# The query and key projection of a channel attention as two row tiles without zero blocks, in a two-bank PSUM area

## The reference

```python
def _L0_conv_ref(x, wq, bq, wk, bk, wv, bv):
    xf = x.reshape(b, c_in, h * w)
    q = jnp.einsum('oc,bcn->bon', wq, xf) + bq[None, :, None]
    k = jnp.einsum('oc,bcn->bon', wk, xf) + bk[None, :, None]
    v = jnp.einsum('oc,bcn->bon', wv, xf) + bv[None, :, None]
    attn = jnp.einsum('bcn,bdn->bcd', q, k) / jnp.sqrt(c)
    attn = jax.nn.softmax(attn, axis=-1)
    attended = jnp.einsum('bcd,bdn->bcn', attn, v)
    return x + attended.reshape(b, c, h, w)
```

## Time and profile before

| | |
|---|---|
| median of 3 runs | 303.3 us (303.17 to 304.55) |
| span of the profiled execution | 301.8 us, 7399 instructions |
| PE | 287.8 us busy (95%) |
| PEld | 183.7 us (61%) |
| DVE | 213.0 us (71%) |
| ACT | 190.4 us (63%) |
| POOL | 53.0 us (18%) |
| DMA | 4.98 MB, mean 16 GB/s |

### The profile page before, as it was taken

How to read it: one execution, slowest core, us unless ns; L and a number is a source line. 1 busy time by engine, 2 the same in 40 slices (tenths; PEclk the granted TensorE clock), 3 DMA queues, 4 the chain that set the end, 5 groups by cost and what they waited for, 6 DMA issues and landing times.

```text
span 301.8 us, 7399 instructions
## 1 busy us (share of the span) xinstructions
PE 287.8 (95%) x2870; PEld 183.7 (61%) x2870; DVE 213.0 (71%) x424; ACT 190.4 (63%) x399; POOL 53.0 (18%) x139
## 2 busy tenths in 40 slices
PE   7798999999999999999999999999999999989995
PEld 3555567567555765575767566675565656657742
DVE  3173984779799788858877827687998996655342
ACT  1268757867886569837685654866975755564332
POOL 0332040400140215010222100301421011011110
PEclk9999999999999999999999999999999999999999
DMA  7300000000000000100010001000000000000001
GB/s 235 140 0 20 0 22 2 2 0 2 0 2 3 3 1 2 35 2 0 3 35 2 3 0 31 8 2 1 2 2 0 21 0 3 17 2 0 2 17 35
DMA packets 3057, 4.98 MB, mean 16 GB/s; under 512 B 336, under 2 KB 2768, under 8 KB 2896
## 3 DMA queue, kind: packets, MB, share of 16 engines
q1 hardware_dynamic: 3024, 4.52, 4.7%
HBM read 3.47 MB, written 1.05 MB: 15 GB/s over the span
## 4 chain that ended last, share of the span: by engine, by line
PE 85%; DVE 5%; ACT 5%; issue 3%; POOL 1%; ACTq 0%; POOLq 0%; DVEq 0%
PE ps_cv L534 22%; PE ps_pair L615 11%; PE ps_yb L494 8%; PE ps_pair L480 7%; PE ps_ma L437 6%; PE ps_ma L464 4%; PE ps_mb L580 3%; PE ps_pair L602 3%; PE ps_pair L570 3%; PE ps_mb L591 3%; PE ps_mb L547 3%; PE ps_mb L388 2%; PE ps_pair L635 2%; PE ps_mb L624 2%; PE ps_yb L374 1%
## 5 line engine op out<-in xcount | busy, mean ns | idle before, releaser
L901 DVE TENSOR_TENSOR sb_wt<-ps_yb,sb_xe 128x512 f32<-128x512 f32 x144 | 94.0, 684 | 26.4 <-PE ps_xb L489 24.9
L534 PE MATMUL ps_cv<-sb_wt,sb_w_x 128*64 128x256 f32 x576 | 77.3, 385 | 0.0
L740 ACT ACTIVATE sb_xe<-ps_xb 128x512 f32<-128x512 f32 x72 | 43.0, 597 | 19.3 <-PE ps_xb L489 19.2
L534 PEld LDWEIGHTS ps_cv<-sb_wt,sb_w_x 128*64 128x64 f32 x576 | 38.2, 136 | 20.2 <-issue 7.5
L615 PE MATMUL ps_pair<-sb_y_pad,sb_par 64*128 64x256 f32 x320 | 37.4, 383 | 0.3 <-ACT sb_gates L799 0.3
L615 PEld LDWEIGHTS ps_pair<-sb_y_pad,sb_par 64*128 64x128 f32 x320 | 30.9, 184 | 5.8 <-issue 2.5
L942 DVE SCALAR_TENSOR_TENSOR sb_dw_acc<-sb_z_pad,sb_par,sb_dw_acc 128x256 f32<-128x256 f32 x56 | 25.2, 480 | 9.4 <-ACT sb_dw_acc L792 5.3
L494 PE MATMUL ps_yb<-sb_hats,sb_sel 32*128 32x512 f16 x144 | 29.8, 383 | 0.7
L1039 POOL TENSOR_TENSOR sb_parts<-sb_hat,sb_parts 128x256 f16<-128x256 f32 (+2 forms) x40 | 23.3, 615 | 38.7 <-ACT sb_parts L710 38.6
L1046 POOL TENSOR_SCALAR sb_sc<-sb_mv 128x1 f32<-128x1 f32 x16 | 3.0, 190 | 142.1 <-DVE sb_mv L936 74.7
L489 PE MATMUL ps_xb<-sb_hats,sb_sel 32*128 32x512 f16 x72 | 27.7, 385 | 0.2 <-ACT sb_hats L719 0.2
(11 more groups left out here) (117 smaller groups left out, 438.4 us busy)
## 6 DMA issues: line engine op xcount, KB each, us to landing
sb_par<-in_par SPq DMA_DIRECT2D x1, 1519.5 KB, 7.7
sb_x_in<-in_x SPq DMA_DIRECT2D x8, 128.0 KB, 2.1
out_y<-sb_y_out SPq DMA_DIRECT2D x8, 128.0 KB, 1.7
sb_par<-in_par SPq DMA_DIRECT2D x1, 397.0 KB, 4.0
sb_par<-in_par SPq DMA_DIRECT2D x1, 192.0 KB, 3.4
sb_par<-in_par SPq DMA_DIRECT2D x1, 128.0 KB, 2.2
sb_sel<-in_sel SPq DMA_DIRECT2D x1, 128.0 KB, 3.9
```

The costliest lines, as they stand in the source:

```text
L534: mm = nc.tensor.matmul(cv[C * b:C * (b + 1), 0:PIX], w_x[n % 2][:, b, h, k, :], wt_of(n, k, h)[:, PIX * b:PIX * (b + 1)], start=(k == 0 a ...
L740: nc.scalar.activation(xe[t % XE][:, :], xb[:, :], ACT.Copy).then_inc(ev("xe_ok"), 1)
L901: nc.vector.tensor_tensor(wt_of(n, k, h)[:, :], yb[h][:, :], xe[t % XE][:, :], ALU.mult)\
```

## The change

`qk` leaves the steps of `mb` and joins those of `pair`. Its matmuls become row tiles: for each half of 128 pixels and each image of the pair, the 64 rows of that image are the stationary operand with all 128 pixels as columns, and the 64 x 128 block of `qk_w` that is not zero is the moving one. The two images write different banks. The count of matmuls stays four, with 128 moving columns each in place of 256. DVE's addition reads both banks, four runs of 128 columns, and writes the same `qk_sb`. The lists of steps are not changed.

```diff
--- before.py
+++ after.py
@@ -123,9 +123,9 @@
 }
 
 
-BANK = {"mb": ("prep", "qk", "attn", "at", "mix", "x1", "qk2", "v2", "et0", "et1", "av", "fuse",
+BANK = {"mb": ("prep", "attn", "at", "mix", "x1", "qk2", "v2", "et0", "et1", "av", "fuse",
                "ff2"),
-        "pair": ("wx0", "wx1", "wx2", "logit", "gate", "scan", "ff")}
+        "pair": ("qk", "wx0", "wx1", "wx2", "logit", "gate", "scan", "ff")}
 DONE = {"prep": "prep_ok", "qk": "qk_ok", "attn": "a_exp_ok", "at": "at_ok", "mix": "mix_ok", "x1": "x1_pad_ok", "wx0": "wx_ok0",
         "wx1": "wx_ok1", "wx2": "wx_ok2", "qk2": "qk2_ok", "v2": "v2_ok", "logit": "exp_ok1", "et0": "et_ok0",
         "et1": "et_ok1", "av": "x3_ok", "gate": "gate_ok", "scan": "scan_ok", "fuse": "x4_ok", "ff": "ff_act",
@@ -382,12 +382,13 @@
             def qk(n):
                 once(pe, n, 1, par_first, 16)
                 pe.wait_ge(x_loaded[n % 2], 16 * ((n + 1) // 2))
-                turn(pe, S, "mb", "qk", n)
+                turn(pe, S, "pair", "qk", n)
                 for h in range(HALVES):
-                    for t in range(2):
-                        mm = nc.tensor.matmul(mb[columns_of(t), 2 * P * h:2 * P * (h + 1)],
-                                              x_in[n % 2][:, P * h + C * t:P * h + C * (t + 1)],
-                                              part("qk_w"), start=True, stop=True)
+                    for b in range(2):
+                        r = slice(C * b, C * (b + 1))
+                        mm = nc.tensor.matmul(pair[:, 512 * b + P * h:512 * b + P * (h + 1)],
+                                              x_in[n % 2][r, P * h:P * (h + 1)],
+                                              part("qk_w")[r, P * b:P * (b + 1)], start=True, stop=True)
                 mm.then_inc(ev("qk_mm"), 1)
 
             def attn(n):
@@ -837,9 +838,9 @@
             def qk(n):
                 dve.wait_ge(ev("qk_mm"), n)
                 once(dve, n, 1, par_first, 32)
-                nc.vector.tensor_tensor(qk_sb[:, :, :, :, :].rearrange("p h b k c -> p h (b k c)"),
-                                        mb[:, :].rearrange("p (h c) -> p h c", h=HALVES),
-                                        part("qk_b").unsqueeze(1).to_broadcast([P, HALVES, 2 * P]),
+                nc.vector.tensor_tensor(qk_sb[:, :, :, :, :].rearrange("p h b k c -> p b h (k c)"),
+                                        pair[:, :].rearrange("p (b h q) -> p b h q", b=2, q=P)[:, :, 0:HALVES, :],
+                                        part("qk_b")[:, 0:P].unsqueeze(1).unsqueeze(1).to_broadcast([P, 2, HALVES, P]),
                                         ALU.add).then_inc(ev("qk_ok"), 1)
 
             def a_max_step(n):
```

## The result

The runs of the changed kernel took 315.7, 317.2, 320.5 and 320.6 us, with a mean granted TensorE clock of 0.989, 0.984, 0.968 and 0.968; beside them the kernel before had a median of 303.9. The ratio, taken over the two shorter runs, is 1.041 with an interval of 1.036 to 1.046; the median of all four is 318.9 us, 4.9% above. In two of the experiments, and in the kernel before beside them, some executions took 1.3 to 3 times as long; they are left out.

The account below looks back on a forecast made before the run. PE was taken to bound the kernel; 1.6 + 0.0 + 1.0 - 0.1 + 5.9 + 1.4 = +9.8 us takes the 301.8 span to 311.6, and 1.5 from span to median gives 313.2 us, range 308.0 to 316.5.

Parts of the forecast that it names:

- the rival on the clock: Clock falls in PE's standstill at image 7, slowing scan.3: 0 to +4.2 us, half +2.1, so 315.3; chance 0.27.
- What bounds the kernel: Whole kernel: 85% of the last-ending chain is on PE, so an added PE wait moves the end unless absorbed later.
- The matmuls' gain: Each projection step (`qk`) on PE: 0.64 us instead of 0.86, a gain of 0.22 us, bounds 0.11 to 0.27.
- Image 1: First projection, `qk.1`: nothing waits for the area, the step is shorter; -0.55 us, bounds -0.3 and -0.9.
- Images 2 and 3: wx0.1 waits for DVE's `qk.2`, `qk.3` for wx0.1's evacuation, wx2.1 for DVE's `qk.3`: +2.15 us, with image 1 +1.6.
- Images 4 and 6: Projections `qk.4` and `qk.6`: area already evacuated, next user not held up; 0.0 us at 4, -0.1 at 6.
- Image 5: `qk.5` waits for ACT to evacuate wx0.3, with s0a.2 and all samples queued behind: +1.0 us.
- Image 7: `qk.7` waits for gate.3's evacuation, scan.3 for DVE's `qk.7` behind six depthwise steps; PE idle some 4.6 us: +5.9 us.
- Image 8: `qk.8` waits for ACT's late evacuation of wx0.7, then wx1.7 waits for DVE's `qk.8`: +1.4 us.
- DVE's add from two banks: DVE's projection add, same 512 elements from two banks: charged nothing, bound above +1.5 us, below zero.
- The rival in which the big wait is absorbed: At image 7, scan.3's wait is not paid: the site costs 1.2 us, not 5.9, so 308.5; chance 0.14.
- the one on the other side: Faster rival: every wait in the `pair` list is met in time, leaving -1.9 us, so 301.4; chance 0.06.

Follow-up runs that it names:

- lower group: Faster runs of the kernel with only images 1, 4 and 6 in the new form, against the kernel before: 302.3 to 302.9 us; the others near 303.8.
- filled kernel: Changed kernel plus idle matmul pairs ahead of PE's long waits (15 at images 2 and 3, 18 ahead of scan.3): 314.5 us median, ratio 1.037.

## Why the prediction was right, point by point

**How near it was.** The direction and the waits came out as forecast, the time less well. 313.2 was forecast, and all four runs took longer; only the shortest, 315.7, lies in the range of 308.0 to 316.5, and the ratio of the two shorter ones times 303.9 is 316.4, 0.1 inside it. Without the high end that the rival on the clock gave, the range would have missed. That the time lies in it is in part luck; the mechanism is not. The sum has a small slip, since 311.6 + 1.5 is 313.1, and the time lies 1.8 above the span of its own execution (320.6 against 318.8), not 1.5.

**What bounds the kernel.** PE's chain (85%) passed every added wait on to the end: the lag grows from line to line of the table, and the only line in which it shrinks, by 0.05, is that of the shorter step of image 6.

**The matmuls' gain**, taken as a step of 0.64 us between 0.59 and 0.75: it measured 0.64, 0.65 and 0.65 at images 5, 7 and 8. The page of the Trainium skill named there, "TensorEngine Tiling (Array Packing)", "Theoretical Speedup", allowed up to twofold, 0.43; in this kernel it is 0.86 / 0.64, a factor of 1.34, the exit to another shape included.

**Image 1**, -0.55: DVE was released 0.56 earlier, and attn.1 starts at 6.38 instead of 7.02 in the kernels with images 1, 4 and 6 alone. This holds where the clock rises at or behind the end of the step, as in the executions compared here; in other executions with the old form DVE was released at 5.23, 5.70 and 5.95, as the clock rose earlier, which leaves less to gain.

**Images 2 and 3**, +2.15: the waits came in the order that was written down (wx0.1, `qk.3`, wx2.1). Less the 0.56 of image 1, the forecast had `qk.3` at 20.74 and wx2.1 at 22.27; they started at 20.74 and 22.33. In the changed kernel the stretch cost 2.53, with the clock's fall in its last 1.3 us; in the kernel with images 2 and 3 alone, clock up, it cost 2.32.

**Images 4 and 6**, 0.0 and -0.1: -0.05 from image 5 to image 7 in the changed kernel. Image 4 can't be read there, since the clock's fall lies ahead of it; in the kernel with images 1, 4 and 6 alone (the execution of the lower group) the lag is -0.62 at wx1.1, -0.64 at ACT's wx0.3 and -0.74 at ACT's gate.3, so -0.02 for image 4 and -0.10 for image 6. **Image 5**, +1.0: 1.00. **Image 7**, +5.9: 5.93, confirmed by the kernel with this image alone and by the one in which DVE's entry was moved. **Image 8**, +1.4: 1.45.

**DVE's add from two banks**, charged nothing: its eight instances have a median of 692 ns against 687 in the kernel before, so the bound of +1.5 was not used.

**Where it was off: the clock.** The forecast of 313.2 had the clock up. The sum of waits behind it (9.8 us) is right within 0.3: 10.1 by the images' prices and 10.1 in the filled kernel's span. But the clock fell in the profiled execution twice, and in no execution of the changed kernel was it up throughout, so that they took 315.7 to 320.6, and three of the four lie above the range. The step that failed is the rival on the clock: it looked for a fall at image 7 alone, priced it at 2.1 (it measured 2.35) and gave it 0.27. Its 315.3 is the nearest to the shortest run, 315.7: a mean clock of 0.989 leaves, by an estimate, 0.011 x 2 x 314 = 6.9 us at half level, as much as the one fall at image 7. It left out the start, where the same working had just placed three standstills of PE, 1.57, 0.88 and 0.88 us long by the idle times of the trace, one behind the other. The fall there cost about 4.5 us, nearly twice as much as the one at image 7; the lower level stayed for 13.7 us, with PE busy in 13.6 of them, instead of 6.9 with PE busy in 4.9. That the standstills bring the falls about is shown as far as this: with idle matmuls in them, seven of eight executions had a mean granted clock of 1.0 and the eighth 0.994, while in the ten without them (four of the changed kernel, six of the one with DVE's entry moved) the mean was 0.939 to 0.994. But the three standstills do not decide alone: images 2 and 3 alone have the same ones, and four of their six runs stayed at 0.998 or above. The Trainium skill, "TensorE: Matmul & The Clock Gate", Part 1, describes a fall behind one long gap between bursts of matmuls, and beside it a clock that swings where PE idles shortly but often between groups of matmuls; the start is like the second, since none of its three gaps is longer than 1.57 us.

The rival in which the big wait is absorbed did not come about, nor did the one on the other side: no evacuation was met in time.

## What to carry to other kernels

When a step moves to another shared area, list for each of its instances the step ahead and the step behind in that area's order, and read from the timeline when the one is evacuated and where the evacuating engine has put the other: the price is there, not in the matmuls. Price a standstill of PE twice, once as a wait and once as the clock that it may cost behind it, and do so for short standstills that stand together as well as for a long one; the second price is paid in some executions and not in others. Where PE is made faster in a place in which it then waits, idle matmuls may be needed to keep what was gained.

## What the runs showed of the hardware beyond what was expected

The granted clock is not the same from run to run of one kernel: its mean is 0.968 to 0.989 in the changed one, and the times follow it. The kernel before is not free of this: in one measurement five of its 21 runs had a mean of 0.992 and took 304.2 to 304.3 us where the median was 303.6, and the kernel with image 7 alone ran at half level for 3.4 us from 10.8, in a part that is the same in both. Taken with the filled kernel's 311.9 at a clock of 1.0, the spans were 313.9 at 0.989, 315.4 at 0.984 and 318.8 at 0.968. At the start, too, it decides: the same binary gives 302.3 to 302.9 or 303.7 to 303.9 us by when the clock rises, and with two pairs of idle matmuls behind `qk.1` all ten runs were of the lower group. The record of the granted clock begins anywhere from 4.0 to 10.1 us in the profiled executions of these kernels, so a difference of some tenths at the start between two single executions says nothing of the kernels.
